# Two feed-forwards: normalised rows split into fp16 halves before they are transposed

## What is computed

```python
# feed-forward 1 (ternary weights: w*q = clip(round(w / s), -1, 1) * s, s = mean |w|), hidden width 1365
h = x + silu(n @ w1q.T) * (n @ w3q.T) @ w2q.T            # n = layernorm(x)
# feed-forward 2 (fp4 weights with group scales), hidden width 1408
g, u = n @ gate, n @ up                                  # n = layernorm(h)
z = (silu(g) * u) @ down
y = h + z / sqrt(mean(z * z) + 1e-6)
```

## Time and profile before

| | us |
| --- | --- |
| median of three executions | 2389.77 |
| the profiled execution | 2391.57 |
| its span, first to last instruction | 2389.8 |
| TensorE busy | 2244.2 (94%) |
| VectorE busy | 1662.7 (70%) |
| ScalarE busy | 1495.3 (63%) |
| GpSimd busy | 1021.4 (43%) |
| mean granted TensorE clock | 0.985 |
| first gate matmul to last one of feed-forward 1 | 977 to 1437 |
| first part matmul of feed-forward 2 to the end | 1801 to 2390 |

### The profile page before, as it was taken

One profiled execution on the slowest core, in us unless ns is written; L12 is line 12 of the kernel. 1 busy time (PEld: TensorE's weight loads), 2 busy tenths in 40 slices (PEclk: granted clock), 3 DMA queues, 4 the chain that ended last, 5 costly groups with the idle time before them and its releaser, 6 DMA issues. The chain is left out here.

```text
span 2389.8 us, 41107 instructions
## 1 busy us (share of the span) xinstructions
PE 2244.2 (94%) x13188; PEld 1128.5 (47%) x13188; DVE 1662.7 (70%) x2931; ACT 1495.3 (63%) x2398; POOL 1021.4 (43%) x1007
## 2 busy tenths in 40 slices
PE   6999999998999996799999999999987999999998
PEld 2333333335666663344444445666652444444443
DVE  6666666665888887456667634666657888888873
ACT  4666666666788785355656425667745666667663
POOL 1222222237777773223324302444434555555552
PEclk9999999999999998799999999999999999999999
DMA  5545445442343211312223212222221011111101
GB/s 146 138 127 135 129 127 135 130 110 66 111 131 114 67 58 36 109 50 79 80 89 93 67 48 84 80 79 79 79 67 40 23 49 40 53 41 45 45 27 53
DMA packets 144300, 194.94 MB, mean 82 GB/s; under 512 B 32773, under 2 KB 76261, under 8 KB 144154
## 3 DMA queue, kind: packets, MB, share of 16 engines
q1 hardware_dynamic: 115642, 154.79, 21.7%
q10 hardware_dynamic: 28512, 38.28, 5.7%
HBM read 125.10 MB, written 42.21 MB: 70 GB/s over the span
## 5 line engine op out<-in xcount | busy, mean ns | idle before, releaser
L341 DVE TENSOR_REDUCE tm_negmax<-tm_s 128x1 f32<-128x512 f32 x512 | 323.3, 679 | 164.7 <-PE tm_s L384 164.4
L303 ACT ACTIVATE tm_prob<-tm_s 128x1024 f32<-128x1024 f32 x256 | 257.6, 1023 | 136.9 <-PE tm_s L404 130.6
L2119 PE MATMUL f_part<-f_xhi,gu 128*128 128x512 f16 x704 | 269.4, 383 | 17.8 <-ACT f_firstg L1922 6.3
L2119 PE MATMUL f_part<-f_xlo,gu 128*128 128x512 f16 x704 | 268.6, 382 | 0.0
L421 PE MATMUL tm_o<-tm_prob,tm_vt 128*64 128x512 f32 x1024 | 255.7, 620 | 0.0
L1888 POOL TENSOR_TENSOR f_firstg<-f_firstg,f_secondg 128x512 f32<-128x512 f32 x88 | 150.7, 1712 | 193.3 <-DVE f_secondg L2006 193.3
L2141 PE MATMUL f_pz<-dn,f_ghi 128*128 128x512 f16 x704 | 214.5, 380 | 5.9 <-ACT f_zc L1954 5.9
L384 PE MATMUL tm_s<-tm_qk 96*128 96x512 f16 x512 | 199.2, 391 | 14.6 <-DMA tm_qk<-tm_xs 14.1
L264 POOL TENSOR_TENSOR tm_hn<-tm_nd,tm_rows 128x1024 f32<-128x1024 f32 x32 | 75.3, 2353 | 291.8 <-DMA tm_rows<-rden 291.8
L404 PE MATMUL tm_s<-tm_qk 98*128 98x512 f16 x512 | 194.2, 382 | 1.6 <-DMA tm_qk<-tm_mrow 1.6
L975 PE MATMUL a_bankB<-a_wo,a_yThi 128*128 128x512 f16 x512 | 158.7, 393 | 4.1 <-DVE a_yTlo L899 4.0
(11 more groups left out here) (190 smaller groups left out, 5668.4 us busy)
## 6 DMA issues: line engine op xcount, KB each, us to landing
tm_qk<-tm_xs SPq DMA_DIRECT2D x384, 64.0 KB, 2.1
tm_xqk<-in_qk ACTq DMA_DIRECT2D x32, 512.0 KB, 4.3
a_hin<-h SPq DMA_DIRECT2D x64, 256.0 KB, 2.7
a_hres<-h SPq DMA_DIRECT2D x64, 256.0 KB, 3.0
h<-a_hout SPq DMA_DIRECT2D x64, 256.0 KB, 2.5
f_hin<-h SPq DMA_DIRECT2D x64, 256.0 KB, 2.7
f_hres<-h SPq DMA_DIRECT2D x64, 256.0 KB, 2.8
tm_vt<-in_vt ACTq DMA_DIRECT2D x32, 256.0 KB, 3.0
```

The lines of the kernel that those rows point to most:

```text
L303: nc.scalar.activation(prob[b][:, 2 * h:2 * h + 2, :], s2[:, i % 2, :, :], ACT.Exp, scale=SCALE).then_inc(exp_done, 1)
L341: nc.vector.tensor_reduce(negmax[u][:, m:m + 1], s1[:, p % BANKS, :], AX.X, ALU.max, negate=True).then_inc(s1_read, 1)
L2119: last = nc.tensor.matmul(part[q % BANKS][:, :], (gate, up)[which][:, j, m * P:(m + 1) * P], xparts[x][u][:, j, :], start=x == 0, stop=x == 1)
```

## The change

In both feed-forwards the split is made before the transposes instead of after them. ScalarE writes the high half of xn (x_high), GpSimd the low half (x_low), both into one fp16 tile, halves. TensorE makes eight fp16 transposes of the two halves into one PSUM bank, now fp16, and ScalarE copies both transposed halves at once (copy_x) into xs, which takes the place of xhi and xlo. VectorE's x_lo is gone, and the identity is fp16. x_high and x_low stand in block m_i-1, copy_x in block m_i+1: in ScalarE's feed-forward 1 list copy_x and then x_high stand at the head of the block, ahead of gate_act. In feed-forward 2 x_high stands at the head, ahead of scale_part, and copy_x behind the first scale_part. x_low stands behind pool_value in feed-forward 1, and at the end of the block in feed-forward 2. xn now waits for x_low of the tile before. Since the fp16 identity is smaller, one region is placed anew (DECODED 28672 to 25728); no work depends on that.

```diff
@@ feed_forward; feed_forward_fp4 has the same functions
-    xhi, xlo = pair("xhi", [P, KT, GT], F16), pair("xlo", [P, KT, GT], F16)
+    xn, halves = sb("xn", [P, DM], F32), sb("halves", [P, 2, DM], F16)
+    xs = pair("xs", [P, 2, KT, GT], F16)
-    px = ps("px", [P, KT * P], F32)
+    px = ps("px", [P, 2 * KT * P], F16)
...
+        def x_low(g, i):
+            if inside(g, GROUPS):
+                t = NT * g + i
+                wait(pool, s["high_done"], t + 1)
+                wait(pool, s["xT_ready"], t)
+                pool.tensor_tensor(halves[:, 1, :], xn[:, :], halves[:, 0, :], ALU.subtract).then_inc(s["low_done"], 1)
...
                 if q is not None:
                     fp4.pool_value(pool, q - 1)
+                if m + 1 in norm_at:
+                    x_low(n + 1, norm_at.index(m + 1))
                 if m + 3 in norm_at:
                     inverse_deviation(n + 1, norm_at.index(m + 3))
...
-        def x_hi(g, i, u):
+        def x_high(g, i):
+            if inside(g, GROUPS):
+                t = NT * g + i
+                wait(act, s["xn_done"], t + 1)
+                wait(act, s["xT_ready"], t)
+                nc.scalar.copy(halves[:, 0, :], xn[:, :]).then_inc(s["high_done"], 1)
+
+        def copy_x(g, i, u):
             if inside(g, GROUPS):
                 wait(act, s["xT_ready"], NT * g + i + 1)
...
-                nc.scalar.copy(xhi[u][:, :, i * P:(i + 1) * P], px[:, :].rearrange("p (j n) -> p j n", j=KT))\
-                    .then_inc(s["xhi_done"], 1)
+                nc.scalar.copy(xs[u][:, :, :, i * P:(i + 1) * P].rearrange("p x j n -> p (x j) n"),
+                               px[:, :].rearrange("p (n c) -> p n c", c=P)).then_inc(s["xs_done"], 1)
 
         def step(n, u, extra=None):
             for m in range(MT):
                 q = slot(n, m)
+                if m - 1 in norm_at:
+                    copy_x(n + 1, norm_at.index(m - 1), 1 - u)
+                if m + 1 in norm_at:
+                    x_high(n + 1, norm_at.index(m + 1))
                 gate_act(n, m, u)
                 if m:
                     hidden_hi(n, m - 1, u)
                 if q is not None:
                     fp4.scalar_high(act, q - 3)
-                if m in norm_at:
-                    x_hi(n + 1, norm_at.index(m), 1 - u)
                 if q is not None:
                     fp4.scalar_prepare(act, q)
...
                 wait(dve, s["rstd_done"], t + 1)
-                wait(dve, s["xT_ready"], t)
+                wait(dve, s["low_done"], t)
                 nc.vector.tensor_scalar(xn[:, :], hin[u][:, :], mv[u][:, 0:1], rstd[u][:, :],
                                         ALU.subtract, ALU.mult).then_inc(s["xn_done"], 1)
...
-                if m in norm_at:
-                    x_lo(n + 1, norm_at.index(m), 1 - u)
...
                 t = NT * g + i
-                wait(pe, s["xn_done"], t + 1)
-                wait(pe, s["xlo_done"], t)
-                for j in range(KT):
-                    last = nc.tensor.transpose(px[:, j * P:(j + 1) * P], xn[:, j * P:(j + 1) * P], ident[:, :])
+                wait(pe, s["low_done"], t + 1)
+                wait(pe, s["xs_done"], t)
+                for x in range(2):
+                    for j in range(KT):
+                        last = nc.tensor.transpose(px[:, (x * KT + j) * P:(x * KT + j + 1) * P],
+                                                   halves[:, x, j * P:(j + 1) * P], ident[:, :])
                 last.then_inc(s["xT_ready"], 1)
@@ feed_forward_fp4, the step of ScalarE
             for m in range(MT):
+                if m + 1 in norm_at:
+                    x_high(n + 1, norm_at.index(m + 1))
                 for which in range(2):
...
                     scale_part(n, m, u, which, 0)
+                    if which == 0 and m - 1 in norm_at:
+                        copy_x(n + 1, norm_at.index(m - 1), 1 - u)
...
                 gate_act(n, m, u)
-                if m in norm_at:
-                    x_hi(n + 1, norm_at.index(m), 1 - u)
```

More of the change, by code:

```diff
@@ L1711, in gate_up @@
                 if m == 0:
-                    wait(pe, s["xlo_done"], NT * (g + 1))
+                    wait(pe, s["xs_done"], NT * (g + 1))
                 wait(pe, s["prod_done"], n - 1)
@@ L1717, in gate_up @@
                         last = nc.tensor.matmul(gu[(m + u) % 2][which][0:rows[m], :],
-                                                weights[:, j, m * P:m * P + rows[m]], xparts[x][u][:, j, :],
+                                                weights[:, j, m * P:m * P + rows[m]], xs[u][:, x, j, :],
                                                 start=c == 0, stop=c == 2 * KT - 1)
@@ L1878, in normalise @@
         def normalise(i):
+            if i >= 0:
+                x_low(0, i)
             if i < NT - 1:
@@ L1908, in normalise @@
         def normalise(i):
-            x_hi(0, i, 0)
+            if i:
+                copy_x(0, i - 1, 0)
+            if i < NT:
+                x_high(0, i)
         def scale_part(g, m, u, which, j):
@@ L1992, in normalise @@
                 row_stats(0, i + 1, (i + 1) // 2)
-            if i >= 0:
-                x_lo(0, i, 0)
         def begin():
@@ L2040, in x_normalised @@
                 wait(dve, s["rstd_done"], t + 1)
-                wait(dve, s["xT_ready"], t)
+                wait(dve, s["low_done"], t)
                 nc.vector.tensor_scalar(xn[:, :], hin[u][:, :], mv[u][:, 0:1], rstd[u][:, :],
                                         ALU.subtract, ALU.mult).then_inc(s["xn_done"], 1)
-        def x_lo(g, i, u):
-            if inside(g, GROUPS):
-                wait(dve, s["xhi_done"], NT * g + i + 1)
-                nc.vector.tensor_tensor(xlo[u][:, :, i * P:(i + 1) * P], px[:, :].rearrange("p (j n) -> p j n", j=KT),
-                                        xhi[u][:, :, i * P:(i + 1) * P], ALU.subtract).then_inc(s["xlo_done"], 1)
         def mean_square(g, i):
```

40 lines of the change are left out of this document (17 added, 23 removed).

## The result

The changed kernel took 2443.52 us (median of four runs, 2437.94 to 2445.14) where the kernel before took 2391.83 beside it (2387.38 to 2394.43): a ratio of 1.0211, with a 95% interval of 1.0193 to 1.0230. The direction was forecast, the size was not: 2420 was said, with 2438 as the upper end. The profiled execution took 2437.94 us, 5.6 us less than the median; its span is 2436.2 us, 46.4 us longer than before. I first account for these 46.4.

What follows compares the result with a forecast made beforehand. TensorE was taken to bound both feed-forwards. The terms 4.7 + 21 + 2.8 + 5.2 - 2 - 1 gave 30.7 us on a median of 2389.77: 2420 us, 1.3% slower, 8-in-10 range 2399 to 2438.

Steps and rivals of the forecast that it cites:

- What bounds the kernel: Both feed-forwards move only with what TensorE does or waits for, except the first group of feed-forward 2.
- TensorE's own work: Transpose steps: eight fp16 transposes take 0.45 us where four float32 took 0.44; below 1 us over 64 tiles.
- rival D: Transposes run at the low clock, 0.9 instead of 0.45 us: +25 us in 56 steady tiles, 2446 us, chance 0.03.
- Prices: New steps: x_high 0.62 us and copy_x 1.02 us on ScalarE, x_low 1.16 us on GpSimd.
- The start: Start of feed-forward 1, first xn to first gate matmul: 16.8 us at 4.05 us a tile, +4.7 us (3 to 6).
- The waits of T: T(n, m), transposes at block m of group n in feed-forward 1, wait for GpSimd's x_low: +21 us (7 to 28).
- Rivals A, B and C: A, T waits a third: 2402, chance 0.11; B, faster by VectorE's relief: 2382, 0.06; C, nothing to be seen: 2390, 0.06.
- The turns: Group turns in feed-forward 1: copy_x behind scalar_prepare's four activations, +1.5 in group 2 and +1.3 in group 4, +2.8 us.
- The clock: Waits of 7.2, 3.9, 3.1 and 2.4 us in feed-forward 1 drop TensorE to 1.2 GHz: +5.2 us (0 to 8).
- The end of attention 1: Last attention steps before feed-forward 2: three gain up to 1 us each, the last tile loses about 1: -2 us.
- Feed-forward 2: First group 0 (-4 to +4), later groups -1 us (-8 to +8); x_high ahead of scale_part partly pays back VectorE's relief.
- Rival E: Feed-forward 2: ScalarE gets 29 us more, bunched ahead of scale_part; 0.5 us for each tile, +14: 2434 us, chance 0.12.

Runs made afterwards that it cites:

- Experiments 4 and 5: In feed-forward 1 of the changed kernel: the former, x_low ahead of pool_value, 2418.39 us; the latter, x_high behind gate_act, x_low still behind pool_value, 2433.83 us.
- Experiment 7: On the kernel of experiment 6, copy_x of feed-forward 1 moved back to block m_i, ahead of scalar_prepare, where x_hi stood: 2391.76 us, 1.0001 of before.
- experiment 6: Changed kernel with both moves, x_low ahead of pool_value in feed-forward 1 and x_high behind gate_act in feed-forward 2: 2402.19 us, 1.0046 of before.
- experiment 8: Feed-forward 1 as before the change, feed-forward 2 as changed but with x_high behind gate_act: 2389.13 us, 0.9990 of before.
- Experiment 10: On the kernel of experiment 8, a 512-column cast of weights that waits for nobody, put where x_high stood ahead of scale_part: 2389.95 us.
- experiment 9: On the kernel of experiment 8, a second, unread copy of 1024 columns on ScalarE ahead of each copy_x in feed-forward 2: 2408.44 us.
- experiments 2 and 3: The former: feed-forward 1 as changed, feed-forward 2 as before, 2432.57 us, 1.0164 of before. For the latter see experiment 3.
- experiment 3: Changed kernel with x_high of feed-forward 2 moved from ahead of scale_part to behind gate_act: 2426.21 us, 17.3 less than the changed kernel.

## Why the prediction was wrong, step by step

The direction and most of feed-forward 1 were right. One term missed a mechanism, feed-forward 2 (put at -1 us, measured +16.6), and one was mis-sized, the clock.

**What bounds the kernel: right.** TensorE was the bound of both stages and stayed it.

**TensorE's own work: right.** Two lines of its timeline of the changed kernel, a transpose step and what follows:

```profile
996.59 0.61 PE L1740 MATMUL f_px<-f_ident,f_halves 128*128 128x128 f16 x8
997.04 1.89 PE L1728 MATMUL f_gu0g<-f_xs,tern 128*128 128x512 f16 x8
```

Eight fp16 transposes take 0.45 us. They ran at the 2.4 GHz level, as 54 of the 56 steps beside matmuls did (0.61 or 0.62 us as drawn; the other two, 1.03 us, stood behind the waits of 4.5 and 7.4 us), and rival D is out. The Trainium skill (TensorE: Matmul & The Clock Gate, Part 4: PE-mode transpose) has the full clock not engage for transposes. Between matmuls the trace does not agree; the four steps of feed-forward 1's start, with nothing else on TensorE, were drawn as 1.01 to 1.04 us and don't tell.

**Prices: right.** x_high, copy_x and x_low by groups (busy us, mean ns, idle time before them):

```profile
L1573 POOL TENSOR_TENSOR f_halves<-f_xn,f_halves 128x512 f16<-128x512 f32 x32 | 37.8, 1183 | 34.9 <-ACT f_halves L1615 34.9
...
L1980 ACT COPY f_xs<-f_px 128x1024 f16<-128x1024 f16 x32 | 32.1, 1003 | 4.1 <-PE f_px L2157 4.1
L1973 ACT CAST f_halves<-f_xn 128x512 f16<-128x512 f32 x32 | 19.8, 618 | 29.7 <-DVE f_xn L2077 27.8 <-PE f_px L2157 1.6
```

1.18, 1.00 and 0.62 us, against 1.16, 1.02 and 0.62. copy_x had no row of its own, and the row of the same length gave it to 2%.

**The start: right.** From the first xn to the first gate matmul 16.35 us (964.84 to 981.19), 16.8 forecast. The cycle was 3.88 and not 4.05 us.

**The waits of T: right, term by term.** 19.9 us against 21, of which 19.9 were for six and 1.0 for small ones: 7.4 (7.2), 4.5 (3.9), 2.7 (3.1), 2.2 (2.4), 1.4 (1.7), 1.4 (1.6) and one small of 0.2. Experiments 4 and 5 show both causes. Rivals A, B and C, which needed 10 us or less there, are out.

**The turns: right.** +2.8 us, in the three waits for f_xs (1.27 + 2.66 + 2.66 against 0.20 + 0.93 + 1.20 + 1.47 for f_xlo). Experiment 7 shows the cause, copy_x behind scalar_prepare. (The two turns that were named gave 1.5 and 1.2 us, where 1.5 and 1.3 were reckoned.)

**The clock: mis-sized.** 5.2 us were forecast. Of the 30.9 us of feed-forward 1 the waits are 22.9, so 8.0 are left; four stretches at the 1.2 GHz level, 14.3 us with TensorE busy, make 7.2 of them. They came with waits of 2.23, 2.66, 4.51 and 7.38 us: the first two began about a us behind the wait, the other two within it. Two windows, the first after T(4,3) and the second after the turn at 1149.37 (the granted clock is the third number from the end):

```profile
1233.00:1237.00 4.00, 4.00 (x13) 1.51 (x11) 1.00 (x2) 1.60 (x2) 0.29 (x1) 0.57 0.58 197
...
1149.00:1152.00 3.00, 2.63 (x13) 1.22 (x14) 1.98 (x3) 2.02 (x4) 0.00 (x0) 1.00 0.82 223
```

A wait of 2.23 us was followed by the low level and one of 2.66 us was not. In the kernel of experiment 6 the same wait of 2.66 us, at the same turn, was:

```profile
1150.00:1153.00 3.00, 3.00 (x9) 1.07 (x7) 2.03 (x3) 1.32 (x3) 0.00 (x0) 0.52 0.94 287
```

The wait for glo, 2.93 us in every one of these profiles, was followed by a granted clock of 0.52 before the change (1441 to 1443 us) and by none of the lower level in experiment 8:

```profile
1445.00:1449.00 4.00, 3.84 (x18) 1.78 (x19) 2.25 (x10) 0.81 (x1) 1.10 (x2) 1.00 0.01 3
```

So for a wait of 2 to 3 us the drop comes in one execution and not in another. The changed kernel has five such waits, two at transposes, two at turns and the one for glo. That fits the gap between its profiled run and its median, too: the profile shows a mean granted clock of 0.983 and 2437.94 us, the other three runs 0.979 to 0.982 and 2442.65 to 2445.14 us. I had counted four drops once each and made the sum against one profiled execution. That the median's missing 5.6 us are such drops is not shown, since the other three runs have no trace, nor in which stage they lie. What decides on a drop is left open.

**The end of attention 1: right sign, mis-sized.** -4.9 instead of -2. I gave three steps up to 1 us each. From xn to xn they gained 2.2, 1.0 and 3.3, and from the last xn to the first part matmul 1.3 us were lost (3.2 to 4.5), where I had 1. So the third step is what was mis-sized.

```profile
1808.19 0.69 DVE L837 TENSOR_TENSOR a_hout<-a_bankB,a_hres 128x512 f32<-128x512 f32 x1 [0.67 <-PE a_bankB L975]
```

VectorE used to stand 3.42 us at x_lo ahead of a_hout; now it stands 0.67 us for TensorE, and a_y comes 3.3 us behind the small operations of the statistics instead of 5.5. At the third step it used to stand 4.14 us at x_lo, and now stands 1.40 us for TensorE.

**Feed-forward 2: this step failed.** I took 0 for the first group and -1 for the others; they were +1.9 and +14.7. The sentence that failed is that x_high ahead of scale_part only pays back VectorE's relief. I had reckoned through exactly this tie in feed-forward 1 (x_high waits for xn, gate_act behind it) and got 7.2 us there; for feed-forward 2 I looked at whether T waits for x_low, found six us of room, and stopped. The trace of before had what was needed. In block 2 of a group, ScalarE's scale_part and VectorE's xn:

```profile
2016.55 0.69 ACT L1922 ACTIVATE f_firstg<-f_part,f_factor 128x512 f32<-128x512 f32 x1 [0.39 <-PE f_part L2119]
2016.72 1.49 DVE L2042 TENSOR_SCALAR f_xn<-f_hin,f_mv,f_rstd 128x512 f32<-128x512 f32 x1
```

xn ended at 2018.2. With x_high (0.62 us) ahead of it, this scale_part, which ran at 2016.55, would start at 2018.8, 2.3 us later. (xn takes 1.5 us here, while one of GpSimd's sum_parts (1.70 us) runs beside it, against 0.54 in the earlier trace rows.) Rival E named the time, 14 us, and the place, ahead of scale_part, but as the cost of work. Experiment 10 parts the two: in the later groups the work there costs nothing and the wait 14 us. E's mechanism is seen in two other places: in the first group, where a cast at that place makes the group as long as x_high there does (and with x_high moved it is 0.9 us shorter than before the change), and for work on top of the change's own, as experiment 9 shows. That E's 14 us met the measured 14.7 is luck: its price of 0.5 us a tile was for another cause.

**The range.** The forecast's own terms were +33.7 in feed-forward 1 (measured +34.7). With feed-forward 2 as it was measured the sum would have been 2422.3 + 1 + 14.7 + 1.9, near 2440, against 2437.94 profiled; from there it is 5.6 us more to the median. That the sum comes so near is partly luck, since the end of attention 1 (3 us too little gain) and the clock (2 us too little loss) cancel in part. The range stopped at 2438 because it took E as an alternative to the clock's and the start's upper ends, though all of them can hold at once.

## What to carry to other kernels

When an instruction is put at the head of an in-order engine's list, reckon its wait, not its length: look for when its input is made and what stands behind it, in each stage that has the same edit, and not only on the path to its own consumer. Here 24 casts of 0.6 us at that place cost nothing where TensorE was the bound, and casts of the same length with a wait for another engine 14 us. A helper's step that the bound engine will wait for goes ahead of work with room to spare. Two moves in the lists of two engines gave back 41 of 52 us.

## What the runs showed of the hardware

A wait of TensorE of 2.66 us, at the same place in its list, was followed by the 1.2 GHz level in one kernel's profile (0.52 from 1150 to 1153 us in experiment 6) and not in another's (1.00 from 1149 to 1152 us in the changed kernel); the waits of 4.5 and 7.4 us came with it in the profiles of the changed kernel and of experiments 2 and 3. The changed kernel's median lies 5.6 us above its profiled execution and that of experiment 3 4.8 us above its own.

VectorE's xn took 0.53 us at 1362.50, as in the earlier trace rows, where it took 0.54, and 1.50 us at 2051.93, with one of GpSimd's sum_parts running beside it. x_low, on average 1.18 us, took 1.60 us at T(6,3). An estimate from the ratio of 1.96 in the Trainium skill (GPSIMD Engine Reference, 3.1 Elementwise) had put x_low at 1.35 us; the group's mean doesn't agree.
